# One decoder layer on one core: the product of q and k, the experts' pipeline, the arms of the branches and the last rows are moved

## The reference, cut to what matters

```
q, k = x @ W_q.T, x @ W_k.T                  # 8 heads of 64
b = (q * k).sum(-1) * SCALE                  # one number for each head and position
a = -softplus(x @ W_alpha_w.T + W_alpha_b).sum over 64
v = x @ W_v.T
y = a scan over the positions of log-domain states of v, decayed by a, fed by b, summed over the heads
x = layernorm(x + y @ W_o.T)

h = relu(x @ proj_in[e].T)                   # 8 experts, 256 -> 512
o = h @ proj_out[e].T                        # 512 -> 256
gate[b, s, e] = sum of ctx where itok == e
x = layernorm(x + sum over e of gate * o)

h = silu(x @ w1.T * s1) * (x @ w2.T * s2)    # 256 -> 1024
h = gelu(h @ h1.T * s); h = gelu(h @ h2.T * s)
x = layernorm(x + h @ w3.T * s3)
```

## Time and profile before

| | |
|---|---|
| median of three runs | 831.17 us |
| the profiled execution | 829.4 us, its span 827.6 us |
| TensorE (PE) busy | 96% of the span |
| VectorE (DVE) busy | 459.3 us, 55% |
| ScalarE (ACT) busy | 306.6 us, 37% |
| GpSimd (POOL) busy | 103.2 us, 12% |
| mean granted clock of TensorE | 0.993 |
| chain that ended last | PE 51%, issue 42%, DVE 3% |

### The profile page before, as it was taken

One profiled execution on the slowest core, in us unless ns is written; L12 is line 12 of the kernel. 1 busy time (PEld: TensorE's weight loads), 2 busy tenths in 40 slices (PEclk: granted clock), 3 DMA queues, 4 the chain that ended last, 5 costly groups with the idle time before them and its releaser, 6 DMA issues.

```text
span 827.6 us, 13038 instructions
## 1 busy us (share of the span) xinstructions
PE 795.5 (96%) x4414; PEld 689.7 (83%) x4414; DVE 459.3 (55%) x1119; ACT 306.6 (37%) x552; POOL 103.2 (12%) x101
## 2 busy tenths in 40 slices
PE   5999899999999998999999989999999999999995
PEld 4877788988899998999899988888888888888884
DVE  3788857774676767667665635323632453245114
ACT  5677632222232313232232226343543264325330
POOL 3565330000220202010020000000000000000000
PEclk9999999999999999999999999999999999999998
DMA  8500000000313130131311000000000000000000
GB/s 330 192 1 0 1 2 2 2 1 25 116 39 103 52 102 27 51 102 51 102 41 49 15 9 1 0 1 1 25 0 0 2 23 0 0 13 13 1 0 27
DMA packets 15587, 31.45 MB, mean 38 GB/s; under 512 B 1584, under 2 KB 6064, under 8 KB 15280
## 3 DMA queue, kind: packets, MB, share of 16 engines
q1 hardware_dynamic: 15536, 30.82, 11.5%
HBM read 28.72 MB, written 2.10 MB: 37 GB/s over the span
## 4 chain that ended last, share of the span: by engine, by line
PE 51%; issue 42%; DVE 3%; ACT 1%; DMA 1%; POOL 1%; POOLq 0%; SPq 0%; DVEq 0%; ACTq 0%
PE bank L728 29%; PE bank L832 21%; PE bank L797 1%; DMA wp_lo_f<-in_wproj 1%; DVE hx_lo L1121 1%; ACT hx_hi L641 1%; POOL rstd L533 0%; DVE masked_late L958 0%; DVE b_tok L973 0%; DVE x_tok L1128 0%; PE bank L804 0%; PE bank L803 0%; DVE vp L983 0%; DVE xT_lo L1116 0%; POOL qk L487 0%
## 5 line engine op out<-in xcount | busy, mean ns | idle before, releaser
L641 ACT ACTIVATE hx_hi<-bank 128x512 fp32r<-128x512 f32 x128 | 76.5, 598 | 267.0 <-PE bank L728 266.8
L832 PE MATMUL bank<-wx_hi,hx_hi 128*128 128x256 f32 x512 | 144.8, 283 | 1.6 <-DVE x_tok L1128 0.9
L832 PE MATMUL bank<-wx_hi,hx_lo 128*128 128x256 f32 x512 | 144.9, 283 | 0.0
L832 PE MATMUL bank<-wx_lo_r,hx_hi 128*128 128x256 f32 x512 | 144.8, 283 | 0.0
L1121 DVE SCALAR_TENSOR_TENSOR hx_lo<-bank,hx_hi 128x512 fp32r<-128x512 f32 x128 | 88.0, 689 | 93.1 <-ACT hx_hi L641 88.2
L728 PE MATMUL bank<-xT_hi,wx_hi 128*128 128x512 f32 x256 | 102.4, 400 | 4.3 <-DVE hx_lo L1121 2.3
L832 PEld LDWEIGHTS bank<-wx_hi,hx_hi 128*128 128x128 f32 x512 | 97.8, 191 | 6.9 <-issue 1.5
L832 PEld LDWEIGHTS bank<-wx_lo_r,hx_hi 128*128 128x128 f32 x512 | 97.8, 191 | 3.9
L728 PE MATMUL bank<-xT_lo,wx_hi 128*128 128x512 f32 x256 | 100.9, 394 | 0.0
L911 PE MATMUL bank<-ha_hi_r,wf_hi_r 128*128 128x512 f32 x256 | 100.0, 391 | 0.0
L911 PE MATMUL bank<-hb_hi_r,wf_hi_r 128*128 128x512 f32 x256 | 99.9, 390 | 0.0
(11 more groups left out here) (147 smaller groups left out, 1344.1 us busy)
## 6 DMA issues: line engine op xcount, KB each, us to landing
stage<-in_wffn SPq DMA_DIRECT2D x44, 256.0 KB, 2.7
wx_lo_f<-in_wx SPq DMA_DIRECT2D x16, 512.0 KB, 4.4
xs_lo_f<-in_xT SPq DMA_DIRECT2D x4, 512.0 KB, 5.4
x_tok<-in_x SPq DMA_DIRECT2D x1, 2048.0 KB, 10.6
out<-x_tok SPq DMA_DIRECT2D x16, 128.0 KB, 1.7
wp_lo_f<-in_wproj SPq DMA_DIRECT2D x3, 512.0 KB, 6.8
ctx_sb<-in_ctx SPq DMA_DIRECT2D x1, 1024.0 KB, 8.7
itok_sb<-in_itok SPq DMA_DIRECT2D x1, 1024.0 KB, 10.5
```

The lines of the kernel that those rows point to most:

```text
L641: act.activation(hx_hi[:, place, c], bank[b][:, :], ACT.Relu).then_inc(s_relu_ok, 1)
L832: mm = pe.matmul(bank[2 + j % 2][:, 0:D], x_, w_, start=(c == 0 and i == 0), stop=(c == XC - 1 and i == 2))
```

## The change

1. **q times k.** ScalarE's copy of k and the semaphore for it are gone. VectorE multiplies `q_sb` with k's bank in `b_sum`, just ahead of the sum over heads. k's bank is free again when that product is done. GpSimd keeps the low parts.
2. **Gates.** In the projections VectorE computes 8 gates instead of 20; the other 12 are computed in the steps of the experts, with scratch for 14 rows.
3. **Experts.** `up` of the next unit now stands with `down` of this one everywhere: from unit 0's four `up` in banks 4 to 7 on, up to unit 31. The first two experts' steps and the three pairs join without a front and a back. VectorE's and ScalarE's orders follow: residuals of the group after the next one and its statistics, scaling and turned halves, each at other places; the weights of expert 2 are split two quarters at a time within the last step.
4. **Arms.** All tests are turned round, so that the arm that runs stands first, right behind the branch. On VectorE everything behind the flag `stepwise` is now written into both arms (`rest`), the one without the step-by-step scan first.
5. **Last rows.** In the last group the output of rows 2 and 3 is made one after the other, and means, root and scaling are done for rows 0 and 1, row 2 and row 3 apart. The last four stores are written out and not a loop.

The diff, cut to its core:

```diff
@@ GpSimd, projections
-                    pool.wait_ge(s_k_out, t + 3)
-                    pool.wait_ge(s_b_red, t + 1)
-                    pool.tensor_tensor(qk[:, j % 2], q_sb[:, j % 2], k_sb[:, j % 2], ALU.mult).then_inc(s_qk_ok, 1)
@@ ScalarE, projections
-                    act.wait_ge(s_k_mm, t + 1)
-                    act.activation(k_sb[:, r], bank[r * 3 + 2][:, :], ACT.Copy).then_inc(s_k_out, 1)
@@ TensorE, projections
-                        pe.wait_ge((s_al_out, s_q_out, s_k_out)[n], t + 1)
+                        pe.wait_ge((s_al_out, s_q_out, s_qk_ok)[n], t + 1)
@@ VectorE, projections
             def b_sum(t, r):
+                dve.wait_ge(s_q_out, t + 3)
+                dve.wait_ge(s_k_mm, t + 1)
+                dve.tensor_tensor(qk[:, r], q_sb[:, r], bank[r * 3 + 2][:, :], ALU.mult).then_inc(s_qk_ok, 1)
                 dve.wait_ge(s_qk_ok, t + 3)
...
-                    if not first and (j < 2 or not last):
+                    if not first and not last and j % 2 == 1:
                         for e in range(2):
-                            gate(t - J, e, masked[:, e])
+                            gate((g - 1) * 2 + j // 2, e, masked[:, e])
@@ TensorE, first two experts
-            for g in range(G):
-                step(g, g < G - 1)
+            for c in range(XC):
+                up(0, 0, 0, c, 0, 4 + c)
+            for n in range(2 * G):
+                for c in range(XC):
+                    if n % 2 == 0 and n < 2 * G - 2 and c == 2:
+                        turned(n // 2 + 1)
+                    e, g = ((n + 1) % 2, (n + 1) // 2) if n < 2 * G - 1 else (0, 0)
+                    up(n + 1, e, g, c, e if n < 2 * G - 1 else 2, c % 2)
+                    down(n, n % 2, n % 2, c, n % 2)
@@ TensorE, pairs
-                for c in range(XC):
-                    up(p * 8, 0, 0, c, p * 2, 4 + c)
...
+                        elif not last:
+                            up(p * 8 + 8, 0, 0, c, p * 2 + 2, c % 2)
                         down(p * 8 + u, u % 2, u // G, c, p * 2 + u // G)
@@ VectorE, first two experts
+                def step(g, front, further):
+                    for c in range(XC):
+                        low(g * 2 + 1, 1, c, c % 2)
+                        if c == 0 and front:
+                            norm_apply(lambda j: group_row(g + 1, j), lambda j: group_row(g + 1, j), g + 1, s_rstd_ok, s_xn_ok)
+                        if c == 2 and front:
+                            halves_x(g + 1)
+                        gated(g * 2, g, c, 0)
+                        for e in range(2, 4):
+                            gate(g * J + c, e, masked_late[:, c * 2 + e - 2])
+                    for c in range(XC):
+                        low(g * 2 + 2, 0, c, c % 2)
+                        if further:
+                            rows_added(g + 2, c)
+                        gated(g * 2 + 1, g, c, 1)
+                        if front:
+                            for e in range(2):
+                                gate((g + 1) * J + c, e, masked_late[:, c * 2 + e])
@@ all engines, here TensorE
-            with pe.If(wide > 0):
+            with pe.If(wide < 1):
+                groups(pe, ffn, True)
+                pe.nop()
+            with pe.Else():
                 pe.wait_ge(s_raw_in, 16)
                 pe.wait_ge(s_f_first, J)
                 groups(pe, ffn, False)
@@ TensorE, output of the network
-                for pair in ((0, 1), (2, 3)):
+                for pair in ((0, 1), (2,), (3,)) if last else ((0, 1), (2, 3)):
@@ VectorE, last group
+                        summed(0)
+                        summed(1)
+                        means((0, 1))
+                        summed(2)
+                        scaled((0, 1), G)
+                        means((2,))
+                        summed(3)
+                        means((3,))
+                        scaled((2,), G + 1)
+                        scaled((3,), G + 2)
@@ VectorE, behind the flag
+            with dve.If(stepwise < 1):
+                rest()
+            with dve.Else():
                 step_path(dve)
...
+                rest()
@@ SyncE, the last four stores
+            for t in range(B - J, B):
+                sp_.wait_ge(s_e_xo, t + 1)
+                sp_.dma_start(out[t], x_tok[:, t]).then_inc(s_out_done, 16)
```

More of the change, by code:

```diff
@@ L542, in ffn @@
                     ln_rstd(s_f_ve, s_f_rstd, g + 2)
-                ln_rstd(s_e_ve, s_e_rstd, g + 1)
-            with pool.If(wide > 0):
-                groups(pool, ffn, False)
+                for part in range(3 if last else 1):
+                    ln_rstd(s_e_ve, s_e_rstd, g + 1 + part, (slice(0, 2), slice(2, 3), slice(3, 4))[part] if last else slice(0, J))
+            with pool.If(wide < 1):
+                groups(pool, ffn, True)
                 pool.nop()
             with pool.Else():
-                groups(pool, ffn, True)
+                groups(pool, ffn, False)
                 pool.nop()
@@ L611, in _, with expert_high @@
             groups_behind(act, project)
-            def expert_high(e, n):
-                for c in range(4):
+            def expert_high(e, n, parts=range(4)):
+                for c in parts:
                     if c % 2 == 0:
@@ L710, in ffn @@
                         norm2_T((g + 1) * J, exact)
-            with act.If(wide > 0):
+            with act.If(wide < 1):
+                groups(act, ffn, True)
+                act.nop()
+            with act.Else():
                 act.wait_ge(s_f_xlo, J)
@@ L715, in _ @@
                 groups(act, ffn, False)
-                act.nop()
-            with act.Else():
-                groups(act, ffn, True)
                 act.nop()
@@ L934, in _ @@
                 groups(pe, ffn, False)
-                pe.nop()
-            with pe.Else():
-                groups(pe, ffn, True)
                 pe.nop()
@@ L993, in project @@
                         b_sum(t - 1, 1 - r)
[L994 removed]
+                    if j == 1 and not first and not last:
                         dve.wait_ge(s_gate_in, 32)
[L996 removed]
+                    if not first and not last and j % 2 == 1:
                         for e in range(2):
[L998 removed]
+                            gate((g - 1) * 2 + j // 2, e, masked[:, e])
                     if j == 2 and last:
@@ L1098, in _ @@
                 dve.wait_ge(s_fall_ve, 2)
-            with dve.Else():
-                dve.nop()
-            dve.sem_inc(s_hlo_ok, 2)
-            dve.sem_inc(s_gated_ok, 2)
-            dve.sem_inc(s_stage_used, 2)
-            dve.sem_inc(s_f_hf, 4)
-            dve.sem_inc(s_f_lo, 3)
-            dve.sem_inc(s_e_mul, 1)
-            def norm_apply(row, dst, g, root, normed):
-                dve.wait_ge(root, g + 1)
-                for j in range(J):
-                    dve.tensor_scalar(dst(j), row(j), mv[:, j, 0:1], rstd[:, j:j + 1], ALU.subtract, ALU.mult).then_inc(normed, 1)
@@ L1263, in _ @@
-            with dve.If(wide > 0):
-                groups(dve, ffn, False)
-                dve.nop()
-            with dve.Else():
-                groups(dve, ffn, True)
-                dve.nop()
+                rest()
 def tiled(w, chunks):
```

335 lines of the change are left out of this document (173 added, 162 removed).

## The result

| | before | changed |
|---|---|---|
| median of the runs | 830.97 us (829.95 to 831.7) | 817.48 us (817.22 to 817.74) |
| profiled execution, its span | 829.4, 827.6 us | 817.22, 815.3 us |
| mean granted clock | 0.993 | 0.998 |

The ratio is 0.9839, 95% interval 0.9821 to 0.9856. Five more runs of the changed kernel gave 817.12 us (816.89 to 817.52). The forecast was 817.5.

What follows compares the result with a forecast made beforehand. TensorE's own work plus its gaps bounds the kernel (795.5 of 827.6 us busy). Terms 1.8 + 7.7 + 1.85 + 1.6 + 1.0 = 13.9 off 829.4 give 815.5; with 1.8 for the median 817.3, stated as 817.5; range 812.5 to 824.5.

Steps and rivals of the forecast that it cites:

- q times k: Projections: with the product on VectorE, TensorE's two gaps before the values close; 1.8 us saved (bounds 0 and 3.0).
- The relief: Projections: with less GpSimd work, VectorE's stretched `sp` and gates shorten, about 1.5 us a group.
- Experts: Experts as one pipeline: front and back go; 7.7 us saved (bounds 3 and 9), 0.8 still lost at the loop's end.
- (a): Behind the flag `stepwise`, VectorE's jump (4.41 us idle): removing it gives nothing, as TensorE runs its idle passes anyway.
- (b): Before the network: TensorE falls through instead of taking a branch of 3426 ns; 1.85 us saved.
- The 1.6 of clock: Start of the network: the half-clock stretch after TensorE's standstill is taken as gone with a shorter gap; 1.6 us.
- The last rows: Tail: one store instead of four after the last scaling, against VectorE's far jump; 1.0 us saved (bounds 2.6 and -0.3).
- 1: Projections: VectorE becomes the bound, a group takes 20.7 us as now and nothing is saved there: 820; chance 0.11.
- 2: Arms give less: the clock falls all the same (1.6), the far jump costs 4.9: 820; chance 0.10.
- 3: Experts: first eight units miss 2.82 us a quarter, 5 of 7.7 us lost: 822.5, or 824; chance 0.09.
- 4: Projections: GpSimd holds up every VectorE instruction with two SBUF inputs, 26.8 us a group: 842; chance 0.03.
- 5: Whole kernel: none of the change shows, since ends only shift into other waits: 831; chance 0.03.

Runs made afterwards that it cites:

- variant 2: The changed kernel with all arms in the old order (wide arm first, flag's arm ahead of an undoubled `rest`): 816.75 us.
- variant 3: The changed kernel with the last group's four rows back in one part (one root, four stores from the loop): 819.91 us.
- variant 4: The changed kernel with experts and gates in the old order, the product still on VectorE: 829.12 us.
- variant 1: The changed kernel with only the product q k back on GpSimd, from ScalarE's copy of k: 814.44 us.
- Experiment 9: The changed kernel with `xs_hi` first in ScalarE's turn and VectorE's `b_sum` ahead of its `a_sum`: 815.97 us.
- experiment 10: The kernel before with only the network's arms in the new order on every engine, the flag's arm as before: 827.74 us.
- variant 5: The changed kernel with ten units of gates back in VectorE's projection loop, in addition to those in the experts: 820.21 us.

## Why the prediction came out right, and where its steps failed

The time is 817.48 for a forecast of 817.5, but this is closer than the steps deserve. Term by term:

**q times k, 1.8 us forecast: failed.** The two gaps were to go; variants 2 and 3, with the product on VectorE and a short start, show the first `up` 0.4 to 0.5 us earlier than before, not 1.8, and the product itself is a loss of 0.6 to 0.8. The four cases, all with short starts, as the time of the first `up`:

| | product on GpSimd | product on VectorE |
|---|---|---|
| gates in the projections | 115.43 (before) | 118.41 (variant 4) |
| 12 of the 20 moved out | 114.21 (variant 1) | 115.04 (variant 2) |

Of the 118.41 some 1.1 are the half clock of experiment 4. All that this part gained comes from the gates. The step that failed is "`xs_hi` of t=11 then comes about 0.5 us earlier", with "so the gap goes if VectorE is not over 0.5 us later than now" built on it. In variant 2, which has the same program there, VectorE was 1.2 us later (`al` at 48.64 for 47.48 before), ScalarE stood behind it, and `xs_hi` came 0.7 us later than before instead of 0.5 earlier. I had added up VectorE's load per group and found it level with TensorE; the load was even less than that (a group lasts 19.86 us, of which VectorE waits 2.0 ahead of `al`). What failed is to judge by load where the order of one engine's instructions sets when another gets its input. It was a price in latency, and I had written it down as zero. Experiment 9 shows it: the same load with `xs_hi` in another place, and the two sums exchanged, has neither of the two gaps.

The relief I counted on is real: `sp` fell from 990 ns to 707, and with the product back on GpSimd it is 993:

```profile
L973 DVE SCALAR_TENSOR_TENSOR sp<-al,sp 128x512 f32<-128x512 f32 x13 | 12.9, 993 | 1.0 <-ACT sp L597 1.0
```

**Experts, 7.7 forecast: right**, 7.8 measured, 8.4 in experiment 4. Inside it the loop's turn lost 0.3, not 0.8, and the start 0.8, not 0.4.

**The arms.** (a) worth nothing under 36 pairs: right, as experiment 2 shows. (b) 1.85 for the branch: right (1.81; 1.86 in experiment 2). The 1.6 of clock: it came (1.62), and experiment 10 shows that in the kernel before the arms alone bring it. But its cause was put too simply: with the new experts the same gap (2.69 us) left the clock at 1.00. Taken alone, the arms are worth 3.4 us by the stages in the kernel before (3.9 by the medians) and 1.3 in the changed one.

**The last rows, 1.0 forecast: mis-sized, 2.6 measured.** The far jump and the near one took 2.8 us together, not 3.7 to 5.2; so VectorE arrives 0.2 us behind SyncE, where I had it 1 us and more behind the stores. SyncE's wait behind its last store, 1.7 to 2.05 us from the issue, covers most of the jump. And the last scaling, which I had as late as before, starts 4.50 us after the last matmul (812.13 - 807.63) instead of 4.93 (822.27 - 817.34), as GpSimd's root of one row takes 0.64 us and that of four took 1.01. The Trainium skill, "Runtime: NRT & Kernel Launch", section "Instruction fetch mechanics", has a taken far branch stop for a fetch. The trace agrees, with 3.4 us (the 3441 ns branch), 4.1, and 2.8 for VectorE's two; from 487 to 492 us of before, around the branch of 3426 ns, a queue of instructions moved two packets of 16 KB, and from 480 to 484 us of the changed kernel, where the arm is fallen into, none. These times hide if another engine's end is as late.

**What made the sum fit.** The terms came to 13.9 and the spans differ by 12.3. The projections gave 1.4 less than forecast and the tail 1.6 more; these cancel. The long start took 2.1 us (the first matmul of the values at 20.82 for 18.70); that the forecast stood at 817.5 is due to the 1.8 us by which I put the median above the profiled execution. I had no reason for these but the runs of before: most of them took 830.4 us or more, and their times suggest that they have a long start and the profiled one a short. Like compared with like, the change is then worth 13.5 us by the medians and 14.4 by the stages (12.3 and 2.1), for 13.9 forecast. So the total was near, by terms that cancel: that is luck in the projections and the tail, and not in the experts and the branch. With a short start the changed kernel should take about 815.2, which none of its nine runs did; variants 1 and 9, with 814.4 and 813.5, did have one.

Of the rivals, 1 was half right: the projections did save next to nothing, but not because VectorE's time is full. 2, 3, 4 and 5 did not come. One sum is off: the upper bounds add up to 18.05 us (3.0 + 9 + 1.85 + 1.6 + 2.6), so the range's lower end is 813 and not 812.5; nothing hangs on it.

## What to carry to other kernels

Before work is moved to an engine with time to spare, look at who waits for what stands behind it there, and put what others wait for first in each turn: here moving two lines (`xs_hi`, and the sum that frees a bank) did what moving 16 products did not. A cover such as idle passes should be cut anew after each change of what it covers; in the changed kernel that was worth more (4.4 us) than the arms (1.3). Look at the granted clock of all runs then, not of one: in the kernel before the same cut gave 1.4 us, and half of its runs had a lower mean clock. Put the arm that is taken first on every engine whose way in is on the path, and look at its way out as well, as it hides behind the last store or does not.

## What the runs showed of the hardware

- The point at which TensorE's products go from 0.43 to 0.23 us apart at the start is about 11.8 us in six of the thirteen traces and 15.9 to 17.3 in seven, and the granted clock of the rows reads 1.00 in both (13 to 15 us: 6 matmuls in one, 10 in the other). The rows of the clock alone would not have shown it:

```profile
13.00:15.00 2.00, 2.00 (x6) 1.52 (x6) 1.32 (x3) 0.63 (x1) 0.00 (x0) 1.00 0.99 410
```

```profile
13.00:15.00 2.00, 2.00 (x10) 1.56 (x9) 1.42 (x3) 0.55 (x1) 0.00 (x0) 1.00 1.02 422
```

- A stop of TensorE (start to start) of 2.64 and 2.66 us ahead of the network was followed by half clock, and so was one of 2.51 ahead of the first output in variants 4 and 5. One of 2.69 us ahead of the network in variant 2 was not, and neither was one of 3.22 us in variant 4 (312.99 to 316.21, 1.00 in the two us behind it). The length of the stop alone does not tell.
- With the product on GpSimd, VectorE's `sp`, which has two SBUF inputs, takes 993 ns in the mean, and 707 without. The Trainium skill, "SBUF — State Buffer", section "Who interferes with whom", says that GpSimd's reads of SBUF hold up such an instruction, and that one with a PSUM input is free of it. The trace agrees: `al` stayed at 684 to 687 in all variants, and the new product, with k in PSUM, took 676 to 678.
